# First batch routed behind the sixth packing by one product, with the setup reordered

## The reference

```
x = x + tanh(g_xattn) * xattn(layernorm(x), ctx, ctx)   # 16 heads of 8, 154 keys, causal mask
x = x + tanh(g_ffn)   * moe(layernorm(x))
# moe: probs = softmax(x @ Wr), top 2 of 8 experts per token, weights normalised over the two
#      rank = cumsum(onehot over tokens and batches); kept if rank <= capacity (160)
#      y_e = gelu(x W1_e + b1_e) W2_e + b2_e ; out = sum over the kept choices of weight * y_e
```

## Time and profile before

| what | us |
|---|---|
| median of 3 runs | 143.41 |
| lowest and highest run | 142.35, 143.93 |
| the profiled execution | 142.3 |
| its span, first to last instruction | 140.2 |
| PE busy | 124.4 |
| DVE busy | 103.2 |
| POOL busy | 84.0 |
| ACT busy | 73.7 |

### The profile page before, as it was taken

The page is one execution under the profiler, slowest core; times in us unless marked ns, Lnnn a source line. Parts: engine busy times, 40 slices in busy tenths (PEclk is TensorE's granted clock), DMA queues, the critical chain, the costliest instruction groups (busy, mean ns, idle before and its releaser), DMA issues.

```text
span 140.2 us, 2241 instructions
## 1 busy us (share of the span) xinstructions
PE 124.4 (89%) x715; PEld 86.4 (62%) x715; DVE 103.2 (74%) x259; ACT 73.7 (53%) x134; POOL 84.0 (60%) x126
## 2 busy tenths in 40 slices
PE   5998988899899999999989989969779999989930
PEld 2443844455455646675369448959579999977620
DVE  5599845948584647377969788974399998999381
ACT  4924667166361447154827778632587678721110
POOL 6679779999999141004285788871067878773000
PEclk9999999999999999999999999999999999999997
DMA  3899880003240000000089411111740101010805
GB/s 97 257 212 222 210 269 23 0 0 99 69 134 0 5 0 0 0 0 2 0 226 314 162 58 39 39 57 55 158 114 10 45 31 43 28 35 26 293 8 150
DMA packets 19018, 12.22 MB, mean 87 GB/s; under 512 B 3381, under 2 KB 16999, under 8 KB 19008
## 3 DMA queue, kind: packets, MB, share of 16 engines
q1 hardware_dynamic: 17344, 9.59, 26.7%
q0 software_dynamic: 1088, 1.86, 4.0%
q10 hardware_dynamic: 576, 0.66, 1.3%
HBM read 7.25 MB, written 5.06 MB: 88 GB/s over the span
## 4 chain that ended last, share of the span: by engine, by line
PE 43%; POOL 17%; DVE 11%; DMA 11%; issue 11%; ACT 2%; SPq 2%; POOLq 1%; DVEq 0%
POOL slots L555 6%; PE turn L873 6%; PE sc L1205 5%; PE av L929 5%; DVE top L1328 4%; PE av L937 4%; PE turn L886 3%; DMA xn_all<-results 3%; PE sc L1221 3%; DMA X<-x 2%; POOL results L587 2%; PE sc L905 2%; PE turn L892 2%; POOL shared L476 2%; DMA parts_all<-slots 2%
## 5 line engine op out<-in xcount | busy, mean ns | idle before, releaser
L1328 DVE TENSOR_REDUCE top<-turn 128x3 fp32r<-128x462 f32 (+2 forms) x44 | 26.2, 606 | 13.8 <-PE turn L873 7.2
L587 POOL DMA_INDIRECT results<-p,result_of x18 | 19.8, 1099 | 12.6 <-DVE p L1630 8.1
L681 ACT ACTIVATE p_all<-sc 128x1024 f32<-128x1024 f32 x16 | 15.5, 1022 | 16.2 <-PE sc L905 16.1
L873 PE MATMUL turn<-shared,q_all 128*128 128x462 f32 (+2 forms) x44 | 20.4, 468 | 2.3 <-DVE top L1328 0.8
L555 POOL DMA_INDIRECT slots<-rows,slot_of x16 | 18.4, 1148 | 5.3 <-issue 5.0
L1205 PE MATMUL sc<-q_all,w_all 128*128 128x320 f32 x96 | 17.4, 320 | 1.2 <-issue 0.8
L752 ACT ACTIVATE late<-sc,B 128x320 f32<-128x320 f32 x32 | 15.0, 523 | 3.5 <-PE sc L1205 3.5
L1205 PEld LDWEIGHTS sc<-q_all,w_all 128*128 128x128 f32 x96 | 14.2, 188 | 2.3 <-issue 2.0
L873 PEld LDWEIGHTS turn<-shared,q_all 128*128 128x128 f32 x44 | 8.3, 189 | 11.4 <-ACT q_pack_all L644 4.7
L546 POOL TENSOR_SCALAR_AFFINE_SELECT p_all<-p_all 128x512 f32<-128x512 f32 x8 | 5.2, 646 | 16.7 <-ACT p_all L681 16.7
L1647 DVE TENSOR_TENSOR shared<-late,shared 128x640 fp32r<-128x640 f32 x16 | 13.1, 821 | 0.3
(11 more groups left out here) (255 smaller groups left out, 283.1 us busy)
## 6 DMA issues: line engine op xcount, KB each, us to landing
W<-w SPq DMA_DIRECT2D x8, 256.0 KB, 3.1
p_all<-w SPq DMA_DIRECT2D x8, 256.0 KB, 5.2
slots<-slot SPq DMA_DIRECT2D x1, 1386.0 KB, 11.0
results<-zeros SPq DMA_DIRECT2D x2, 512.0 KB, 9.7
parts_all<-slots SPq DMA_DIRECT2D x5, 198.0 KB, 2.9
X<-x SPq DMA_DIRECT2D x2, 256.0 KB, 3.6
xn_all<-results SPq DMA_DIRECT2D x2, 256.0 KB, 3.9
xn_all<-results ACTq DMA_DIRECT2D x2, 256.0 KB, 4.2
```

Source lines behind the costliest of these rows:

```text
L587: nc.gpsimd.indirect_dma_start(out=results, out_offset=bass.IndirectOffsetOnAxis(ap=result_of[0:m, e, n:n + 1], axis=0), in_=y[0:m, e % 2, ...
L681: act.activation(p0[:, t, heads, :], sc[:, heads, :], ACT.Exp, scale=SCALE).then_inc(sc_free, 1)
L873: mm = pe.matmul(o, qT[:, 0, b, qt * P:qt * P + P], kTr[:, b, h0:h0 + nh, 0:keys], start=True, stop=(qt >= 2), skip_group_check=True)
L1328: dve.tensor_reduce(top[:, qt, h0:h0 + nh, 3 * HD], ps[:, 0:nh * keys].rearrange("p (h k) -> p h k", h=nh), AX.X, ALU.max).then_inc(turn_f ...
```

## The change

The maxima are cut into 40 units instead of 44. Units of tiles 1 to 3 now have three heads each throughout (0-2, 4-6, 7-9, 10-12, 13-15), and head 3 of the three tiles is one unit. Five are in the setup. The cuts inside a step stay as they were. So in step 0 the units of heads 7 to 9 come behind `pack(1)`, and in step 1 the unit of heads 10 to 12 of tile 3 comes behind `pack(2)`: for head 7 of tiles 1 to 3 and heads 10 and 11 of tile 3, first batch, `top` still holds zero when it is packed, and zero is the shift.

The first batch of x is loaded in two halves, on two queues. DVE clears `slot0`, takes the statistics of the first batch alone, writes the ones beside the values (which POOL wrote), and signals every normalised tile. The second batch's statistics come behind the keys' first products, its normalised rows behind the setup's maxima, its turning behind `pack(0)`, its queries inside step 0. ACT writes the high part of the keys itself. POOL's order changes, and `keys_for_max` of the first batch is cut in two. The fills of PE fall from 12 and 4 products to 3 and 3.

`router(1)` stands in step 4. In step 5 ACT copies the turned attention rows, and one product per tile with the gated `WO` and `WOR` side by side gives both rows and logits behind `pack(6)` (`project_first`). DVE adds them, takes the statistics and chooses. In step 6, behind `pack(7)`, come the counting product, the normalised rows and `place(0)`. The last step's later keys are set to zero by DVE instead of POOL. All eight slot writes of the first batch are issued ahead of `root` of the second.

```diff
+def units_of_maxima(b, i):
+
+    first = [(b, (0,), 4 * i, 4, P)]
+    if i == 0:
+        return first + [(b, (qt,), 0, 3, C) for qt in range(1, QT)] + [(b, tuple(range(1, QT)), 3, 1, C)]
+    starts = ((), (4, 7), (10,), (13,))[i]
+    return first + [(b, (qt,), h0, 3, C) for h0 in starts for qt in range(1, QT)]
...
-        shares = (7, 8, 6, 6, 6, 5, 5, 1)
+        FIRST_TURNED, FIRST_PLACED = 5, 6
+        ROUTER = {2: "weights", 3: 0, 4: 1}
...
+        shares = (5, 7, 6, 6, 6, 5, 4, 1)
         maxima_first = maxima_todo[:shares[0]]
-        FIRST_HEADS = 6
+        FIRST_HEADS = 4
+        NEXT_HEADS = 10
...
+            sp.dma_start(X[:, 0:2, :], x_d[:, 0:2, :]).then_inc(x_in[0], 16)
...
+            sp.dma_start(X[:, QT:NT, :], x_d[:, QT:NT, :]).then_inc(x_in[2], 16)
...
+            pool.wait_ge(cleared, 1)
+            packing(pack_k, [kp for kp, qp in PRODUCTS]).then_inc(pack_ready, 1)
+            pool.tensor_copy(identb[:, :], identf[:, :]).then_inc(consts2, 1)
+            root((0, QT), 1)
...
-            pool.tensor_copy(identb[:, :], identf[:, :]).then_inc(consts2, 1)
-            root((0, QT), 1)
-            root((QT, NT), 2)
-
-            pool.wait_ge(cleared, 1)
-            packing(pack_k, [kp for kp, qp in PRODUCTS]).then_inc(pack_ready, 1)
+            pool.wait_ge(cleared, 2)
             packing(pack_q, [qp for kp, qp in PRODUCTS]).then_inc(pack_ready, 1)
...
+            pool.wait_ge(kT_ready, 1)
+            keys_for_max(0, FIRST_HEADS, NEXT_HEADS)
+
+            root((QT, NT), 2)
...
             step(pool.memset(mask_k1[:, :], 0.0))
-            for j in range(4):
-                m = mask_k1[32 * j:32 * j + 32, :]
-                step(pool.affine_select(out=m, in_=m, compare_op=ALU.is_ge, fill=NEG, base=0,
-                                        pattern=[[1, 32]], channel_multiplier=-1))
+            pool.affine_select(out=ident4[:, :, :], in_=ident4[:, :, :], compare_op=ALU.not_equal, fill=1.0, base=0,
+                               pattern=[[0, 4], [-1, 32]], channel_multiplier=1)
+            step(pool.affine_select(out=mask_k1[:, :], in_=mask_k1[:, :], compare_op=ALU.is_ge, fill=NEG, base=0,
+                                    pattern=[[1, 32]], channel_multiplier=-1))
             pool.memset(ones[:, :], 1.0).then_inc(consts3, 1)
...
+                if b == 0:
+                    keys_for_max(0, NEXT_HEADS, H)
...
+            for g in range(NG - 1):
+                if g == FIRST_PLACED:
                     root(blocks[0], 3)
...
-            for t in range(QT // 2):
+            for t in range(QT):
                 send(0, t)
             root(blocks[1], 4)
-            for t in range(QT // 2, QT):
-                send(0, t)
             for t in range(QT, NT):
...
+            act.dma_start(X[:, 2:QT, :], x_d[:, 2:QT, :]).then_inc(x_in[1], 16)
...
+            act.activation(kT_part[:, 0], sc1[:, 0:B * CP].rearrange("p (b k) -> p b k", b=B),
+                           ACT.Copy).then_inc(kT_ready, 1)
...
-            turned_rows(1)
             place_values()
-            high_queries(1)
 
...
             pack(0)
-            act.wait_ge(small_in, 64)
-            act.activation(gate[:, :], G[:, :], ACT.Tanh).then_inc(gate_ready, 1)
+            turned_rows(1)
...
                     act.activation(p0[:, t, heads, :], sc[:, heads, :], ACT.Exp,
                                    scale=SCALE).then_inc(sc_free, 1)
+                if g == 0:
+                    high_queries(1)
                 act.wait_ge(sc_full, 3 * g + 3)
                 act.activation(p1[:, t, :], sc1[:, 0:Q1], ACT.Exp, scale=SCALE).then_inc(sc_free, 1)
+                if g == 0:
+                    act.wait_ge(small_in, 64)
+                    act.activation(gate[:, :], G[:, :], ACT.Tanh).then_inc(gate_ready, 1)
+                if g == FIRST_TURNED:
+                    act.wait_ge(first_turned_ps, 1)
+                    act.activation(attnT, turn[turns.index(("turned", 0)) % 2][:, :], ACT.Copy).then_inc(first_turned, 1)
+                if g == FIRST_PLACED:
+                    exp_of_difference(0)
                 if g + 1 < NG:
                     pack(g + 1)
                 if g >= 2 and g % 2 == 0:
                     copy_values(g // 2 - 1)
-                if g == NG - 1:
-                    exp_of_difference(0)
 
...
-            def add_zeros(ps, n):
-
-                for _ in range(n):
-                    pe.matmul(ps.rearrange("p (n d) -> p n d", n=2), identb[:, :],
-                              zeros[:, :].bitcast(BF16).unsqueeze(1).to_broadcast([P, 2, 2 * P]), start=False,
-                              stop=False, skip_group_check=True)
...
+            def turn_first():
+
+                pe.wait_ge(turn_free, use_of["fold", 1])
+                ps = bank((first_turned, 1))
+                for t in range(QT):
+                    mm = pe.transpose(ps[:, t * P:t * P + P], attn[:, t].rearrange("p n d -> p (n d)"), identf[:, :])
+                mm.then_inc(first_turned_ps, 1)
+
+            def project_first(h):
+
+                pe.wait_ge(first_turned, 1)
+                pe.wait_ge(gated_ready, 1)
+                ps = bank()
+                for c in range(2):
+                    q = (2 * h + c) * P
+                    mm = pe.matmul(ps[:, c * (D + E):(c + 1) * (D + E)], attnT[:, q:q + P], gated, start=(c == 0),
+                                   stop=True, skip_group_check=True)
+                mm.then_inc(turn_full, 1)
...
             pack_keys(0)
-            pe.wait_ge(consts2, 1)
+            pack_keys(1)
+            pe.wait_ge(consts2, 2)
             pe.wait_ge(kTr_first, 1)
             pe.wait_ge(q_high, 1)
-            maxima(maxima_first[0:2])
-            pack_keys(1)
+            maxima(maxima_first[0:1])
+            pack_keys(2)
+            maxima(maxima_first[1:2])
+            pack_keys(3)
             maxima(maxima_first[2:3])
-            pack_keys(2)
-            maxima(maxima_first[3:4])
-            pack_keys(3)
-            maxima(maxima_first[4:5])
-            turn_rows(1)
-            maxima(maxima_first[5:6])
             project_values()
-            maxima(maxima_first[6:])
-            queries(1)
+            maxima(maxima_first[3:])
             pe.wait_ge(pack_ready, 2)
             pe.wait_ge(q_ready, 1)
             pack(0)
-            pe.wait_ge(consts3, 1)
+            pe.wait_ge(v_ready, 5)
+            turn_rows(1)
             for g in range(NG + 1):
-                if g == 0:
-                    pe.wait_ge(kTr_ready, 1)
-                if g == 2:
-                    pe.wait_ge(kTr_ready, 2)
...
+                if g < 3:
+                    pe.wait_ge(kTr_ready, g + 1)
...
                     pe.wait_ge(k_ready, 1)
-                    pe.wait_ge(q_ready, 2)
+                    pe.wait_ge(consts3, 1)
                 if g < NG:
                     last_scores(g)
+                if g == 0:
+                    queries(1)
                 if g in FOLD:
                     fold_parts(FOLD.index(g))
                 maxima(maxima_beside(g, 2))
                 if g == 5:
                     fill(av[:, :], 3)
-                if g == 6:
-                    add_zeros(av[:, :], 4)
-                for when, k, n in BESIDE:
-                    if when == g:
-                        post(k, n)
+                if g == FIRST_TURNED:
+                    turn_first()
                 if g + 1 < NG:
                     pack(g + 1)
                 maxima(maxima_beside(g, 3))
+                if g == FIRST_TURNED:
+                    for h in range(2):
+                        project_first(h)
+                if g == FIRST_PLACED:
+                    count(0)
                 if g == 1:
-                    pe.wait_ge(v_ready, 5)
+                    pe.wait_ge(ones_placed, 1)
+                    pe.wait_ge(q_ready, 2)
                 if 1 <= g <= NG:
                     values(g - 1)
...
+            def add_first(h):
+
+                tiles = slice(2 * h, 2 * h + 2)
+                ps = bank()[:, 0:2 * (D + E)].rearrange("p (t c) -> p t c", t=2)
+                dve.tensor_tensor(x1[:, tiles, :], ps[:, :, 0:D], X[:, tiles, :], ALU.add)
+                dve.tensor_tensor(logits[:, tiles, :], ps[:, :, D:D + E], given[:, tiles, :],
+                                  ALU.add).then_inc(turn_free, 1)
...
+            dve.memset(pack_k_raw, 0.0).then_inc(cleared, 1)
             dve.memset(pack_q_raw, 0.0).then_inc(cleared, 1)
-            dve.wait_ge(x_in[0], 16)
-            statistics((0, QT), X)
-            dve.wait_ge(x_in[1], 16)
-            statistics((QT, NT), X)
-            layernorm((0, QT), X, xn, xn_ready)
-            dve.wait_ge(consts2, 1)
-            dve.tensor_reduce(minus_one[:, :], minus_raw[:, :, :], AX.XY, ALU.add).then_inc(minus_ready, 1)
+            step(dve.memset(slot0[:, :], 0.0))
+            dve.memset(slot0[:, D:D + 1], FAR).then_inc(slot_zeros, 1)
```

(50 more changed lines are left out.)

265 lines of the change are left out of this document (103 added, 162 removed).

## The result

The changed kernel takes **154.82 us** (median of 4 runs, 153.98 to 157.24) against 142.91 (4 runs, 142.35 to 143.93): a ratio of 1.084, 95% interval 1.076 to 1.092. I had forecast 141.8. The profiled execution took 154.14 and spans 152.0 us, 11.8 more than before.

What follows compares the result with a forecast made beforehand. PE (43% of the chain) and POOL (17%) bound different stretches. Setup and loop +0.55, last mask -0.3, root +0.4 and table -2.2 sum to -1.55 us: 141.8 against the median of 143.4, range 138.3 to 144.3.

Steps and rivals of the forecast that it cites:

- rival C: Behind the loop: eight slot writes hold back the second root, deciding from a pitch of 1.56 us; 145 to 147, chance 0.10.
- rival D: Setup: with fewer PE fills the clock drops to 1.2 GHz, 3 us more on the chain, 144.8; chance 0.06.
- Loop start: End of the setup: the last transpose ends near 17.6 us, so the loop starts 2.0 early (1.2 to 2.9).
- Step 0: Loop's first step: `low_queries(1)` waits for ACT's copy and holds the units before `pack(1)`; cost 1.35 us (0.3 to 1.9).
- Step 1: Loop: units grow to 2872 columns and `pack(2)` waits for a unit directly ahead; cost 0.8 us (0.3 to 1.2).
- Steps 2 and 3: Loop: 154 more columns and the unit of three tiles; cost 0.2 us (0 to 0.5).
- Steps 5 and 6: Loop's end: PE loses 3.4 us of products but waits for DVE before the last packing; -0.7 us (-2.0 to +0.3).
- The last mask: Behind the last exponentials: DVE does the first half while ACT is at the second; -0.3 us (-0.5 to +0.3).
- The root: Second batch's root on POOL, behind all eight first-batch writes, and DVE waits for it; +0.4 us (0 to 1.3).
- The table: Table read back before expert 3: complete some 4 us earlier, DVE's 2.53 wait goes; -2.2 us (1.6 to 2.5 early).
- Rival B: At the table: the wait only hid another, so the gain of 2.2 shrinks to 0.5, 143.5 us; chance 0.10.
- Rival A: The loop keeps the setup's gain, its waits having been there anyway; 138.4 to 140, put at 139 us; chance 0.29.

Runs made afterwards that it cites:

- e3: The changed kernel with POOL's keys of 16 heads cut into four operations of four heads: 153.39 us, ratio 1.078 to the kernel before.
- e1: The changed kernel with POOL waiting for all eight normalised tiles before its large keys: 146.62 us, ratio 1.033 to the kernel before; profiled run 143.29.
- e8: e7 and e5 together, six units ahead of the first packing and the root ahead of the eighth write: 141.34 us, ratio 0.991 to the kernel before.
- e10: e8 without POOL's wait for the second batch's normalised rows: 148.39 us, ratio 1.038 to the kernel before.
- e4: e1 with `low_queries(1)` moved behind the units that `pack(1)` waits for: 145.86 us, ratio 1.018 to the kernel before.
- e7: e4 with six units of maxima ahead of the first packing instead of five, one fewer in step 0: 142.36 us, ratio 0.992 to the kernel before.
- e9: e8 with `router(1)` back in step 5: 140.47 us, ratio 0.982 to the kernel before, the fastest version.
- e5: e4 with the second batch's root between the seventh and eighth slot write of the first batch: 143.06 us, 0.996 of the kernel before.

## Why the prediction was wrong, step by step

**The failed step** is in the setup: "Then DVE normalises the second batch, 1.1, and the last transpose ends near 17.6." I took 1.1 from the first batch's rows. The list of POOL that I had made ("POOL's shorter list", constants at 15.5) came in time, its `ones` at 14.14. What I did not do is to lay that list beside DVE's rows: the change puts these 1.1 us of DVE under 7.1 us of `tensor_tensor` on POOL. It took 6.80. The trace of before had a sign of it. There the second batch's own rows took 1.50, not the first batch's 1.11 that I used, beside POOL's short selections:

```profile
10.87 1.50 DVE L1321 TENSOR_SCALAR xn_all<-X,mean_var,rstd 128x128 f32<-128x128 f32 x4
...
11.17 1.12 POOL L447 TENSOR_SCALAR_AFFINE_SELECT pack_q<-pack_q 128x128 fp32r<-128x128 f32 x3
```

Three of these rows took 0.52 instead of 0.34, and each of them ended 0.08 behind one of the three selections. I knew the rule: the Trainium skill (SBUF — State Buffer, "SBUF: two separate sides") says that whichever of the two starts first, a DVE operation in a 2-port mode or with two SBUF inputs or a GpSimd operation, has the shared port pair for the whole instruction. I weighed it for the slot writes alone. The trace agrees with it for the rows: one took 4.49 us beside one POOL operation of 4.31, in e3 one row came through behind each piece, and in e1, with POOL waiting, none was held. Which of the rule's two cases these rows are, with one full-width input and two scalars per partition, no run here shows. At the writes, where I had put it (rival C), it did not decide: the pitch beside DVE's selections was 1.40 (single writes 0.97 to 1.43), under C's threshold of 1.56.

**The clock** was rival D at 0.06, with the price of 3 us. It came, but as a consequence: "PE's fills … cost nothing while the clock holds" was wrong as soon as PE had nothing to do for 4 us. Its price here was larger than mine, 5.5 us in steps 0 and 1 against e1, since behind the thin step 0 it was lost a second time. Against e8 the loss of 13.5 us divides by e10 into 7 for the rows with the first loss of the clock, and another 6.4 (154.8 - 148.4) for step 0, the second loss up to 42 to 44, the root and one unit, which were only undone together.

**Loop start**: 2.0 early predicted; 2.55 in e1, where rows and clock are as I assumed. The term was right but for this.

**Step 0**: +1.35 predicted, +1.43 in e1, +3.98 in the changed kernel at half clock. The mechanism is as described: there DVE idles 2.60 ahead of `low_queries(1)` for ACT's copy, in e1 1.41. e4 shows the size: moving that one operation takes 0.73 of it; that the rest is the hand-over of the units I argue, no run shows it. **Step 1**: +0.8 predicted, +1.20 in e1; no run separates the larger units from the new wait of `pack(2)`. **Step 4**: +0.9 predicted, +0.77 measured.

**Steps 2 and 3**: +0.2 predicted; +0.24 after, +1.0 in e1, +0.55 in e7. The difference is the failed step once more, in small. At the start of step 2 DVE forms `std`, a product of 128x8 with both inputs in SBUF. From e1, and the last line from after:

```profile
32.10 1.28 POOL L538 TENSOR_TENSOR w_all<-W,w_all 128x512 fp32r<-128x512 f32 x1
...
32.49 0.91 DVE L1579 TENSOR_TENSOR std<-mean_var,rstd 128x8 f32<-128x8 f32 x1
...
44.37 0.16 DVE L1578 TENSOR_TENSOR std<-mean_var,rstd 128x8 f32<-128x8 f32 x1
```

It takes 0.16 in the changed kernel, with POOL idle, 0.48 in e7 and 0.91 in e1, where it ends 0.02 behind POOL's operation, and step 2 takes 6.88, 7.19 and 7.65. So the wait of e1 wasn't free: it made POOL's work later and put it beside this product, for 0.75 us.

**Steps 5 and 6**: -0.7 predicted, +0.01 measured in four kernels. The timeline of PE in step 6, after:

```profile
74.74 0.73 PE L884 MATMUL turn<-q_all,pack_q 128*128 128x512 f32 x2
76.45 0.66 PE L890 MATMUL turn<-identr,top 128*128 128x128 f32 x4 [0.98 <-DVE top L1322]
```

PE waits for DVE ahead of the last packing, as I had said; only the waits are longer. In the two steps PE is busy 12.21 us instead of 13.57, DVE 10.69 instead of 8.81. What PE was spared is now idle time, so the gain is nil. In the profiles of e8 and e9 this stretch even costs the clock (e8: PE 1.03 of 2 us busy at 62 to 64, clock 0.50 at 66 to 68), once more an effect that I had not priced.

**The last mask**: -0.3 predicted, nothing measured. values(7) start 3.35 behind scores(7), before 3.39. **The root**: +0.4 predicted, with 1.3 as the bound; +1.35 measured. I had its input at 77.0 - 65.0 = 12.0 behind the scores of step 7, and it was there at 89.79 - 78.99 = 10.8, as before (10.73). The term was mis-sized by this. e5 shows that one write moved behind the root is enough to undo it at the root; at expert 3 that was worth 0.2. **The table**: -2.2 predicted; from the root to the products of expert 3 it is -2.54. Rival B did not come in the changed kernel. But the wait is not gone as I wrote, 0.70 is left, and in e7 1.50: the read of the table landed 4.5 us after its issue here, 5.3 in e7 and 3.8 before.

**The sum** at full clock, as e1 has it: +1.85 at scores(7) (I had +0.55), of which 0.75 is `std`'s, then -1.45 to expert 3 (36.65 to 35.20; I had -2.1). That is +0.40 where I had -1.55. The span of e1 is 1.0 longer than before. The 0.6 between them lies behind expert 3 and isn't the change's: there the changed kernel takes 37.5 us, as before, and e1 38.1. So even without its failed step the forecast was some 2 us too low; the change as designed gained nothing. **Rival A** is refuted by e1: of the 2.55 that the setup gained, 1.12 were left at scores(1) and nothing at scores(2). It took four edits on top (the wait, the place of `low_queries(1)`, the sixth unit, the root) to keep a part of it, and `router(1)` in its old place to come to e9's 1.8%.

## What to carry to other kernels

When an edit moves a DVE operation on SBUF, lay it beside what GpSimd does at its new time, not only beside its own inputs: three GpSimd `tensor_tensor` operations turned 1.1 us into 6.8, the longest of them alone held one row for 4.49. Where they collide, a wait on the engine with slack gave back 11 us in the profiled execution; look then at what its delayed work stands beside (0.75 us in step 2). Cutting the long operation helps only by its pieces. And a stretch in which PE idles has a second price behind it, at the lower clock, which shows as a busy PE: read the clock's row before the busy rows.
